# The last batch's projections in another order, over 89 steps instead of 64

## The chip, the cores and the metric

The kernel runs on one core of a Trainium2 chip. That core has five engines that run their own instruction streams and meet only at semaphores: TensorE (PE; its weight loads are listed apart as PEld), VectorE (DVE), ScalarE (ACT), GpSimd (POOL) and SyncE (SP), which here issues DMAs. The metric is the device time of one execution in microseconds, lower is better.

## The reference

One transformer block with adaptive modulation, in float32: 4 batches of 1024 tokens, width 512, 16 heads of 32.

```python
ada = silu(c) @ Wada.T + bada                      # six vectors of 512 for each batch
h = rmsnorm(x, g1) * (1 + scale_msa) + shift_msa
q, k, v = split(h @ Wqkv.T + bqkv)                 # 16 heads of 32
q, k = rmsnorm(q, gq) * 32**-0.5, rmsnorm(k, gk)   # over the 32 of a head
x = x + gate_msa * ((softmax(q @ k.T) @ v) @ Wproj.T + bproj)
h = rmsnorm(x, g2) * (1 + scale_mlp) + shift_mlp
x = x + gate_mlp * (gelu(h @ Wfc1.T + bfc1) @ Wfc2.T + bfc2)
```

## The kernel before, in words

There are three stages: a short setup, the attention, and then output projection and MLP. The change is in the attention alone, which writes its result to DRAM for the third stage.

**The steps.** The attention is a loop over 256 steps, the same on every engine (`for L in range(START, AFTER)`; 18 steps ahead of step 0 only prepare). The 16 heads are taken in 4 groups of 4 (`g`). A batch is 64 steps, a group of heads 16, and the two halves of its queries 8 each; in this text a half is such a run of 8 steps, and `j` (0 to 7) is the place in it, one block of 128 keys. Batch 3, the last, is attended in steps 192 to 255. In a step TensorE makes the scores of 4 heads in two pairs (L456), ScalarE takes the exponential of each pair into one of 3 `probs` buffers (L616, two instructions of 128x1024), TensorE multiplies the `probs` of the step before with `v` (L469), and VectorE adds the `probs` of the step before to a running sum (L681, 128x2048; seven times in a half, none for the first block alone). At `j` = 1 TensorE sums the rows of the finished half (`row_sums`, L486) and waits for its seventh addition. From there the sums go through DRAM, are inverted on VectorE at `j` = 5 (L701), come back by DMA (L403), and at `j` = 0 the half's output is scaled (`output`, L697).

**The projections.** The products of a batch's `h` with the weights of q, k and v are not a stage of their own: they are put between the scores. They are 24 products for each batch: 8 tiles of `v` (`v_of(t, steps)`) and 16 units (`k_of(g, half, steps)`, `q_of(g, half, steps)`), one for each group, half, and q or k. Each product is 12 matmuls of 512 columns into the one PSUM bank `gemm` (L521 for units, L534 for `v`). `placed` lays them out one after the other: a product of 3 steps gets 4 of its 12 matmuls in each step, one of 2 steps 6, one of 6 steps 2. `fill(L, 0)` issues the first part of a step's share between the two pairs of scores, `fill(L, 1)` the second part behind them. In a new product `fill` first waits until VectorE has copied the previous one out of the bank (`gemm_free`).

**What follows a unit.** One step behind the end of a unit VectorE copies it to `raw` with its bias (`raw_out`, L712; a tile of `v` is copied by `v_out`, L722), ScalarE squares it (L597), the step after that TensorE adds the squares up for each head (`sum_squares`, L493, moved on by a step where another user of its bank stands), ScalarE takes logarithm and inverse root (L587, L591), and VectorE makes the normalised unit in two parts (`make_parts`, L761, L767, L769), at the END of its step, behind that step's addition. `raw_out`, `v_out`, `output` and the inversion stand AHEAD of the addition. SyncE stores the parts to DRAM (L359) and loads them, spread for the scores, at places that the group and the half fix (L381). Every engine works its stream in order.

**The input.** Eight tiles of `x` for each batch are normalised and turned, one every 8 steps, the last of batch 3 at step 170; ScalarE and GpSimd split the turned tile in two parts two steps later (L607, L653). A product of the second half of the tokens needs all 8 tiles.

**The plan.** `PLAN` is a list of numbers that sets all of this; from `FILL`, `UNIT_END` and `VOUT` every engine derives its stream. For the batches 2 and 3 it begins 48 steps ahead of the batch and lasts 64 steps, so the products of batch 3 lie in the steps 144 to 207, and the steps 208 to 255 have none.

Of the kernel before, what the change touches and what calls it, by code (L numbers as in the profile page):

```python
# [23 lines left out]
B, T, D = 4, 1024, 512  # L24
# [11 lines left out]
BSTEPS = NG * STEPS  # L36
# [18 lines left out]
def v_of(t, steps):  # L55
    return "v", 0, t, steps


def k_of(g, half, steps):
    return "k", g, half, steps  # L60


def q_of(g, half, steps):
    return "q", g, half, steps


def placed(step, b, products):

    plan = []
    for kind, g, x, steps in products:  # L70
        plan.append((step, steps, b, kind, g, x))
        step += steps
    return plan


def first_half(v_steps, steps):

    return [p for g in range(NG) for p in (k_of(g, 0, steps), q_of(g, 0, steps), v_of(g, v_steps))]


SECOND_HALF = [k_of(0, 1, 3), q_of(0, 1, 3), v_of(4, 2), v_of(5, 2), k_of(1, 1, 3), v_of(6, 2), q_of(1, 1, 3),
               k_of(2, 1, 3), v_of(7, 2), q_of(2, 1, 3), k_of(3, 1, 3), q_of(3, 1, 3)]
START = -18
PLAN = placed(-14, 0, [v_of(0, 1), v_of(1, 1), v_of(2, 1), k_of(0, 0, 1), q_of(0, 0, 1), v_of(3, 1), v_of(4, 1),
                       k_of(0, 1, 1), q_of(0, 1, 1), v_of(5, 1), v_of(6, 1), v_of(7, 1)])
# [2 lines left out]
PLAN += placed(25, 1, [v_of(0, 2), v_of(1, 2), k_of(0, 0, 2), q_of(0, 0, 2), k_of(1, 0, 2), v_of(2, 2), q_of(1, 0, 2), k_of(2, 0, 2),  # L88
                       q_of(2, 0, 2), v_of(3, 2), k_of(3, 0, 3), q_of(3, 0, 3), k_of(0, 1, 2), q_of(0, 1, 2), v_of(4, 2), v_of(5, 2),
                       k_of(1, 1, 3), v_of(6, 2), q_of(1, 1, 3), k_of(2, 1, 2), v_of(7, 2), q_of(2, 1, 3), k_of(3, 1, 3), q_of(3, 1, 3)])  # L90
for b in range(2, B):
    PLAN += placed(BSTEPS * b - 48, b, first_half(2, 3) + SECOND_HALF)

FILL = {step + i: (kind, b, g, x, i, steps) for step, steps, b, kind, g, x in PLAN for i in range(steps)}
UNIT = [(b, g, kind, x) for _, _, b, kind, g, x in PLAN if kind != "v"]
# [31 lines left out]
for step, n in FIN_AT.items():  # L127
    b, g, kind, half = UNIT[n]
# [1255 lines left out]
```

## Time and profile before

| | us |
|---|---|
| median of 3 runs (1860.57 to 1865.57) | 1863.95 |
| the profiled execution | 1864.95 |
| its span in the trace | 1863.2 |
| first exponential of step 144, and of step 208 | 650.25, 877.94 |
| start of the last pair of exponentials | 999.4 |
| TensorE busy, of the span | 1760.5 (94%) |
| VectorE busy | 1101.3 (59%) |
| ScalarE busy | 921.3 (49%) |

A step can be read from the trace by the start of its first exponential (ACT L616): from one such start to the next is the step's length. An engine's busy share over the whole span is an average of three stages. For the attention it says little, since the third stage keeps TensorE busy and the others less so.

### The profile page before, as it was taken

The page shows a single profiled execution, that of the slowest core. Times are in us where ns is not written, and L with a number is a line of the kernel's source. Part 1 is how long each engine was busy: PE and PEld are TensorE (multiplying, and loading weights), DVE is VectorE, ACT ScalarE, POOL GpSimd, SP SyncE. Part 2 cuts the span into 40 slices and gives each one's busy share as a digit, 9 for nine tenths or more (in the row PEclk, how much of TensorE's full clock was granted, in tenths as well). Part 3 has the DMA queues.
Part 4 walks back from the last instruction along what each step waited for, and adds up shares of the span by engine and source line. Part 5 has one row for each costly group of instructions (what it writes and reads, how often), then busy time and mean ns, then how long its engine had stood idle before and what let it go on. Part 6 is the DMA issues. An engine that isn't in the chain of part 4 may idle for free. (4 is left out here: it accounts for less than half of the span.)

```text
span 1863.2 us, 23267 instructions
## 1 busy us (share of the span) xinstructions
PE 1760.5 (94%) x8368; PEld 1139.4 (61%) x8368; DVE 1101.3 (59%) x1343; ACT 921.3 (49%) x1110; POOL 363.3 (19%) x296
## 2 busy tenths in 40 slices
PE   3899899999999999999995799999999999999998
PEld 1555454555555555544231577888888787878786
DVE  4578878888898888878785654223232414232311
ACT  2277577777777777777885432222121222122221
POOL 1100100010110110000000432324241424233331
PEclk7999999999999999999997799999999999999999
DMA  5555535556555555454563331202020201001000
GB/s 184 153 146 142 138 107 139 137 138 157 132 132 144 135 144 128 126 133 137 132 134 103 116 102 40 63 6 62 17 62 17 62 17 51 28 30 44 6 29 23
DMA packets 137611, 176.69 MB, mean 95 GB/s; under 512 B 33668, under 2 KB 58244, under 8 KB 137528
## 3 DMA queue, kind: packets, MB, share of 16 engines
q1 hardware_dynamic: 122472, 158.79, 32.1%
q10 hardware_dynamic: 15056, 16.81, 2.8%
q8 instruction: 50, 0.82, 0.2%
q14 instruction: 33, 0.27, 0.1%
HBM read 124.63 MB, written 50.92 MB: 94 GB/s over the span
## 5 line engine op out<-in xcount | busy, mean ns | idle before, releaser
L616 ACT ACTIVATE probs<-scores,shift 128x1024 f32<-128x1024 f32 x512 | 549.7, 1115 | 195.6 <-PE scores L456 191.8
L681 DVE TENSOR_TENSOR sums<-sums,probs 128x2048 f32<-128x2048 f32 x192 | 444.5, 2315 | 45.0 <-ACT probs L616 40.7
L456 PE MATMUL scores<-q_stack,k_stack 128*128 128x512 f32 x1024 | 345.7, 423 | 6.6 <-ACT probs L616 6.5
L456 PEld LDWEIGHTS scores<-q_stack,k_stack 128*128 128x128 f32 x1024 | 169.6, 188 | 254.4 <-ACT probs L616 133.3
L1148 PE MATMUL acc<-w_hi,act_parts 128*128 128x512 f32 x1024 | 317.4, 391 | 0.0
L469 PE MATMUL pv<-probs,v 128*32 128x512 f32 x2048 | 274.3, 608 | 0.4 <-ACT probs L616 0.4
L1111 POOL TENSOR_TENSOR act_parts<-act_full,act_parts 128x512 fp32r<-128x512 f32 x128 | 169.6, 1325 | 501.7 <-ACT act_parts L1062 501.0
L1055 ACT ACTIVATE act_full<-up,f_bias 128x512 f32<-128x512 f32 x128 | 88.3, 690 | 337.7 <-PE up L1165 317.0
L1148 PEld LDWEIGHTS acc<-w_hi,act_parts 128*128 128x128 f32 x1024 | 190.7, 188 | 38.6
L1165 PE MATMUL up<-z_hi,w_hi 128*128 128x512 f32 x512 | 201.5, 394 | 5.1 <-POOL z_lo L1098 5.1
L1165 PE MATMUL up<-z_lo,w_hi 128*128 128x512 f32 x512 | 200.3, 391 | 0.0
L1165 PE MATMUL up<-z_hi,w_lo 128*128 128x512 f32 x512 | 200.2, 391 | 0.0
L1148 PE MATMUL acc<-w_lo,act_parts 128*128 128x512 f32 x512 | 199.4, 389 | 0.0
L1223 DVE TENSOR_TENSOR y_next<-proj,p_bias 128x512 f32<-128x512 f32 x28 | 19.3, 690 | 297.2 <-PE proj L1126 297.2
L1062 ACT ACTIVATE act_parts<-act_full 128x512 fp32r<-128x512 f32 x128 | 81.2, 635 | 222.1 <-PE acc L1148 221.0
L521 PE MATMUL gemm<-h_hi,wqkv_hi 128*128 128x512 f32 x256 | 103.9, 406 | 14.4 <-issue 11.6
L1165 PEld LDWEIGHTS up<-z_hi,w_hi 128*128 128x128 f32 x512 | 96.9, 189 | 25.5 <-POOL z_lo L1098 5.5
L469 PEld LDWEIGHTS pv<-probs,v 128*32 128x32 f32 x2048 | 41.1, 108 | 114.7 <-ACT probs L616 62.2
L658 POOL TENSOR_TENSOR x_inv<-x_sqc,minus_half 128x1 f32<-128x1 f32 x32 | 17.6, 551 | 475.9 <-DVE x_sqc L733 475.9
L1165 PEld LDWEIGHTS up<-z_lo,w_hi 128*128 128x128 f32 x512 | 97.0, 189 | 20.1
L1165 PEld LDWEIGHTS up<-z_hi,w_lo 128*128 128x128 f32 x512 | 96.8, 189 | 20.4
L1148 PEld LDWEIGHTS acc<-w_lo,act_parts 128*128 128x128 f32 x512 | 96.1, 188 | 20.2
(134 smaller groups left out, 2092.9 us busy)
## 6 DMA issues: line engine op xcount, KB each, us to landing
parts_scratch<-parts SPq DMA_DIRECT2D x64, 512.0 KB, 3.1
k_stack<-parts_scratch SPq DMA_DIRECT2D x128, 256.0 KB, 4.9
q_stack<-parts_scratch SPq DMA_DIRECT2D x128, 256.0 KB, 5.1
xt<-in_x SPq DMA_DIRECT2D x32, 256.0 KB, 2.9
heads_out<-o_out SPq DMA_DIRECT2D x32, 256.0 KB, 4.7
out<-result SPq DMA_DIRECT2D x32, 256.0 KB, 2.0
inverse<-inverse_scratch SPq DMA_DIRECT2D x124, 64.0 KB, 2.0
heads<-heads_out SPq DMA_DIRECT2D x30, 256.0 KB, 3.3
```

The lines of the kernel that those rows point to most:

```text
L456: mm = nc.tensor.matmul(scores[p][:, i, :], k_stack[s][:, h, j * P:(j + 1) * P], q_stack[half][:, h, :], start=True, stop=True)
L469: mm = nc.tensor.matmul(pv[hh % NH][h * DH:(h + 1) * DH, :], v[b % 2][:, j, (g * HG + h) * DH:(g * HG + h + 1) * DH], probs[l % RING][:, h ...
L521: mm = nc.tensor.matmul(gemm[:], w[:, k, at:at + P], h[:, k, c], start=(n == 0), stop=(n == len(terms) - 1))
L616: nc.scalar.activation(probs[L % RING][:, 2 * p:2 * p + 2, :], scores[p][:], ACT.Exp, bias=small["shift"][:]).then_inc(exp_done, 1)
L658: nc.gpsimd.tensor_tensor(x_inv[:, t:t + 1], x_sqc[:, t:t + 1], small["minus_half"][:, 0:1], ALU.pow).then_inc(inv_done, 1)
L681: nc.vector.tensor_tensor(sums[:], a[:], probs[l % RING][:], ALU.add).then_inc(added, 1)
L1055: nc.scalar.activation(act_full[m % 2][:], up[m % 2][:], ACT.Gelu_apprx_tanh, bias=f1_bias[:, m:m + 1]).then_inc(gelu_done, 1)
L1062: nc.scalar.activation(act_parts[m % 2][:, 0, :], act_full[m % 2][:], ACT.Copy).then_inc(act_hi, 1)
L1111: nc.gpsimd.tensor_tensor(act_parts[m % 2][:, 1, :], act_full[m % 2][:], full(act_parts[m % 2][:, 0, :]), ALU.subtract).then_inc(act_lo, 1)
L1148: mm = nc.tensor.matmul(acc[t][:], act_parts[m % 2][:, b, t * P:(t + 1) * P], w2[a][:, m, :], start=(m == 0 and i == 0), stop=(m == NM - 1 ...
L1165: mm = nc.tensor.matmul(up[m % 2][:], w1[a][:, k, m * P:(m + 1) * P], z[b][:, k, :], start=(k == 0 and i == 0), stop=(k == KT - 1 and i == 2))
L1223: nc.vector.tensor_tensor(yt, proj[:], p_bias[:], ALU.add).then_inc(proj_moved, 1)
```

## The change

The batches 0, 1 and 2 keep their plan. Batch 3 gets one of its own. It begins at the same step (144), takes the products in another order, gives 12 tiles and units other numbers of steps, leaves the steps 171 and 172 free, and ends at step 232 instead of 207. The tiles of `v` come earlier (the last ends at step 181, before at 198), and the units of the groups 2 and 3 now lie at the steps 194 to 232, inside the batch. From step 188 on all units of q and the first unit of k of group 2 are six steps long.

```diff
-for b in range(2, B):
-    PLAN += placed(BSTEPS * b - 48, b, first_half(2, 3) + SECOND_HALF)
+PLAN += placed(2 * BSTEPS - 48, 2, first_half(2, 3) + SECOND_HALF)
...
+PLAN += placed(3 * BSTEPS - 48, 3, [k_of(0, 0, 3), v_of(0, 3), q_of(0, 0, 3), v_of(1, 3), v_of(2, 3), v_of(3, 3), k_of(1, 0, 3),
...
+PLAN += placed(3 * BSTEPS - 19, 3, [k_of(0, 1, 3), q_of(0, 1, 3), v_of(7, 3), q_of(1, 0, 3), k_of(1, 1, 3), q_of(1, 1, 6),
+                                    k_of(2, 0, 6), q_of(2, 0, 6), k_of(2, 1, 3), q_of(2, 1, 6),
+                                    k_of(3, 0, 3), q_of(3, 0, 6), k_of(3, 1, 3), q_of(3, 1, 6)])
```

In the whole, counted from the two plans for the 112 steps 144 to 255:

| matmuls of products in a step | steps before | steps after |
|---|---|---|
| 6 | 16 | 6 |
| 4 | 48 | 45 |
| 2 | 0 | 36 |
| 0 | 48 | 25 |

Both columns hold 288 matmuls. What moves on TensorE shows in two pieces. `scores0` and `scores1` are the two pairs of scores, `gemm` the bank of the products, `aux` that of the sums, `pv` the output. Before, TensorE at step 203:

```order
L456 MATMUL scores0<-q_stack1,k_stack0 128x512 x2
L521 MATMUL gemm<-h_lo,wqkv_hi 128x512
L521 MATMUL gemm<-h_hi,wqkv_lo 128x512
L456 MATMUL scores1<-q_stack1,k_stack0 128x512 x2
L521 MATMUL gemm<-h_hi,wqkv_hi 128x512
L521 MATMUL gemm<-h_lo,wqkv_hi 128x512
L493 MATMUL aux<-squares,head_ones 128x512
L469 MATMUL pv1<-probs1,v1 32x512 x4
```

After, TensorE at the steps 218 and 219 (its lines are six higher in number):

```order
L462 MATMUL scores0<-q_stack1,k_stack1 128x512 x2
L527 MATMUL gemm<-h_hi,wqkv_hi 128x512
L462 MATMUL scores1<-q_stack1,k_stack1 128x512 x2
L527 MATMUL gemm<-h_lo,wqkv_hi 128x512
L475 MATMUL pv1<-probs1,v1 32x512 x4
L462 MATMUL scores0<-q_stack1,k_stack1 128x512 x2
L527 MATMUL gemm<-h_hi,wqkv_lo 128x512
L462 MATMUL scores1<-q_stack1,k_stack1 128x512 x2
L527 MATMUL gemm<-h_hi,wqkv_hi 128x512
L499 MATMUL aux<-squares,head_ones 128x512
L475 MATMUL pv1<-probs2,v1 32x512 x4
```

A step of a six-step unit holds one matmul of the product behind each pair of scores, where a step of a three-step unit holds two.

On VectorE the neighbours of the copies change. `raw` is the copy of a unit, `parts` its normalised form, `sums` the addition. Before, VectorE at the steps 200 to 205:

```order
L697 TENSOR_TENSOR o_out<-pv1,inverse 128x512
L681 TENSOR_TENSOR sums<-sums,probs1 128x2048
L761 SCALAR_TENSOR_TENSOR raw0<-norms,raw0 128x512
L767 TENSOR_SCALAR parts<-raw0 128x512
L769 SCALAR_TENSOR_TENSOR parts<-raw0,parts 128x512
L712 TENSOR_SCALAR raw1<-gemm,qk_bias 128x512
L681 TENSOR_TENSOR sums<-probs2,probs0 128x2048
L681 TENSOR_TENSOR sums<-sums,probs1 128x2048
L681 TENSOR_TENSOR sums<-sums,probs2 128x2048
L712 TENSOR_SCALAR raw0<-gemm,qk_bias 128x512
L701 RECIPROCAL compact<-compact 128x16
L681 TENSOR_TENSOR sums<-sums,probs0 128x2048
```

After, VectorE at the steps 200 to 206:

```order
L718 TENSOR_SCALAR raw0<-gemm,qk_bias 128x512
L703 TENSOR_TENSOR o_out<-pv1,inverse 128x512
L687 TENSOR_TENSOR sums<-sums,probs1 128x2048
L687 TENSOR_TENSOR sums<-probs2,probs0 128x2048
L687 TENSOR_TENSOR sums<-sums,probs1 128x2048
L687 TENSOR_TENSOR sums<-sums,probs2 128x2048
L767 SCALAR_TENSOR_TENSOR raw0<-norms,raw0 128x512
L773 TENSOR_SCALAR parts<-raw0 128x512
L775 SCALAR_TENSOR_TENSOR parts<-raw0,parts 128x512
L707 RECIPROCAL compact<-compact 128x16
L687 TENSOR_TENSOR sums<-sums,probs0 128x2048
L718 TENSOR_SCALAR raw1<-gemm,qk_bias 128x512
```

Before, the three instructions of `make_parts` are at step 200 and the next copy at step 202, and no addition stands between them, since step 201 has none. After, they are at step 204, and an inversion and an addition stand between them and the copy of step 206.

## Rows read from the trace of the kernel before

**Rows 1.** Windows: length; busy us and count by engine; PEclk, DMA share, GB/s

```profile
650.25:877.94 227.69, 226.96 (x1170) 115.78 (x1168) 189.51 (x177) 171.44 (x189) 11.79 (x8) 1.00 0.51 133
877.94:999.50 121.56, 114.83 (x620) 38.31 (x622) 101.13 (x59) 105.27 (x105) 0.00 (x0) 0.99 0.50 119
```

**Rows 2.** Waits of TensorE from 650.25 to 877.94: in total, times, longest

```profile
PE scores L456 <- ACT probs L616: 0.7, 1, 0.7
```

**Rows 3.** Timeline of ScalarE, steps with products: start, length, instructions, [idle before]

```profile
794.38 2.18 ACT L616 ACTIVATE probs<-scores,shift 128x1024 f32<-128x1024 f32 x2 [1.05 <-PE scores L456]
...
797.86 2.20 ACT L616 ACTIVATE probs<-scores,shift 128x1024 f32<-128x1024 f32 x2 [0.69 <-PE scores L456]
...
802.59 2.12 ACT L616 ACTIVATE probs<-scores,shift 128x1024 f32<-128x1024 f32 x2 [2.02 <-PE scores L456]
805.62 2.12 ACT L616 ACTIVATE probs<-scores,shift 128x1024 f32<-128x1024 f32 x2 [0.91 <-PE scores L456]
808.66 2.12 ACT L616 ACTIVATE probs<-scores,shift 128x1024 f32<-128x1024 f32 x2 [0.92 <-PE scores L456]
...
832.90 2.12 ACT L616 ACTIVATE probs<-scores,shift 128x1024 f32<-128x1024 f32 x2 [0.41 <-PE scores L456]
...
836.80 2.12 ACT L616 ACTIVATE probs<-scores,shift 128x1024 f32<-128x1024 f32 x2 [1.05 <-PE scores L456]
```

**Rows 4.** Timeline of ScalarE, steps 224 to 229, without products

```profile
922.49 4.24 ACT L616 ACTIVATE probs<-scores,shift 128x1024 f32<-128x1024 f32 x4 [0.44 <-DVE sums L681]
...
928.03 4.25 ACT L616 ACTIVATE probs<-scores,shift 128x1024 f32<-128x1024 f32 x4 [0.82 <-PE scores L456]
...
932.72 4.25 ACT L616 ACTIVATE probs<-scores,shift 128x1024 f32<-128x1024 f32 x4 [0.44 <-PE scores L456]
```

**Rows 5.** Timeline, steps 187 to 189: addition, copy, next product's first weights

```profile
807.77 2.29 DVE L681 TENSOR_TENSOR sums<-sums,probs 128x2048 f32<-128x2048 f32 x1 [0.74 <-ACT probs L616]
...
809.98 0.75 DVE L712 TENSOR_SCALAR raw<-gemm,qk_bias 128x512 f32<-128x512 f32 x1
...
811.19 0.19 PEld L534 LDWEIGHTS gemm<-wqkv_hi,h_hi 128*128 128x128 f32 x1
```

**Rows 6.** Timeline, steps 212 to 218: VectorE, and who waited for it

```profile
890.83 0.68 DVE L761 SCALAR_TENSOR_TENSOR raw<-norms,raw 128x512 f32<-128x512 f32 x1
...
892.74 0.25 DVE L701 RECIPROCAL compact<-compact 128x16 f32<-128x16 f32 x1
892.90 7.02 DVE L681 TENSOR_TENSOR sums<-sums,probs 128x2048 f32<-128x2048 f32 x3
901.11 0.69 DVE L697 TENSOR_TENSOR o_out<-pv,inverse 128x512 f32<-128x512 f32 x1 [1.19 <-DMA inverse<-inverse_scratch]
901.72 2.28 DVE L681 TENSOR_TENSOR sums<-sums,probs 128x2048 f32<-128x2048 f32 x1
904.05 1.93 PE L486 MATMUL aux<-sums,ones 128*32 128x512 f32 x8 [2.38 <-DVE sums L681]
908.43 4.25 ACT L616 ACTIVATE probs<-scores,shift 128x1024 f32<-128x1024 f32 x4 [1.78 <-DVE sums L681]
```

**Rows 7.** Timeline, steps 29 and 30: a copy behind `make_parts`

```profile
218.38 1.12 ACT L616 ACTIVATE probs<-scores,shift 128x1024 f32<-128x1024 f32 x1 [0.79 <-PE scores L456]
219.46 0.68 DVE L722 TENSOR_TENSOR v<-gemm,v_bias 128x512 f32<-128x512 f32 x1
...
220.19 0.50 PE L521 MATMUL gemm<-h_hi,wqkv_hi 128*128 128x512 f32 x1 [1.93 <-DVE v L722]
...
225.62 1.12 ACT L616 ACTIVATE probs<-scores,shift 128x1024 f32<-128x1024 f32 x1 [2.78 <-PE scores L456]
```

**Rows 8.** Windows over two places behind a wait (columns of Rows 1)

```profile
904.00:907.40 3.40, 3.35 (x16) 0.59 (x16) 1.28 (x1) 0.60 (x1) 0.00 (x0) 0.51 0.67 158
...
221.40:224.80 3.40, 3.40 (x13) 0.93 (x12) 2.94 (x2) 1.12 (x1) 0.00 (x0) 0.50 0.34 112
```

**Rows 9.** Timeline: the split of batch 3's last tile at step 172

```profile
751.66 2.68 POOL L653 TENSOR_TENSOR h_lo<-h_full,h_hi 128x512 fp32r<-128x512 f32 x1 [7.79 <-ACT h_hi L607]
```

More of the change, by code:

```diff
@@ L90 @@
                        k_of(1, 1, 3), v_of(6, 2), q_of(1, 1, 3), k_of(2, 1, 2), v_of(7, 2), q_of(2, 1, 3), k_of(3, 1, 3), q_of(3, 1, 3)])
-for b in range(2, B):
-    PLAN += placed(BSTEPS * b - 48, b, first_half(2, 3) + SECOND_HALF)
+PLAN += placed(2 * BSTEPS - 48, 2, first_half(2, 3) + SECOND_HALF)
+PLAN += placed(3 * BSTEPS - 48, 3, [k_of(0, 0, 3), v_of(0, 3), q_of(0, 0, 3), v_of(1, 3), v_of(2, 3), v_of(3, 3), k_of(1, 0, 3),
+                                    v_of(4, 2), v_of(5, 2), v_of(6, 2)])
+PLAN += placed(3 * BSTEPS - 19, 3, [k_of(0, 1, 3), q_of(0, 1, 3), v_of(7, 3), q_of(1, 0, 3), k_of(1, 1, 3), q_of(1, 1, 6),
+                                    k_of(2, 0, 6), q_of(2, 0, 6), k_of(2, 1, 3), q_of(2, 1, 6),
+                                    k_of(3, 0, 3), q_of(3, 0, 6), k_of(3, 1, 3), q_of(3, 1, 6)])
 FILL = {step + i: (kind, b, g, x, i, steps) for step, steps, b, kind, g, x in PLAN for i in range(steps)}
```

## The prediction

> **What bounds the kernel now.** I read the windows first, to see which engine is full in the stretch that the change touches, then TensorE's waits there, then ScalarE's timeline, because the start of a step's first exponential dates every step. The steps 144 to 207, with products, take 227.69 us, and TensorE is busy for 226.96 of them; the steps 208 to 255, without, take 121.56, with TensorE at 114.83 at almost full clock [rows 1]. A busy TensorE is not a full one, so the waits decide: in the first stretch it waited once, for 0.7 us [rows 2]. There it sets the pace, and each matmul costs its time.
>
> Prices of steps, from start to start [rows 3]: with 4 matmuls of products 805.62 to 808.66, 3.03 (mean with the step before, 802.59 to 805.62); with 6, 794.38 to 797.86, 3.48. So a matmul more costs 0.45/2 = 0.225 us. A sum of squares adds 0.87 (832.90 to 836.80 is 3.90, less 3.03), a row sum 1.25 (797.86 to 802.59 is 4.73, less 3.48). Without products two steps take 932.72 - 928.03 = 4.69, so 2.345 each, and with a row sum in one of them 928.03 - 922.49 = 5.54, 0.85 more [rows 4]. TensorE's own work in an empty step would be 3.03 - 4 x 0.225 = 2.13; the 0.2 above it is the loop of scores, exponential and next scores.
>
> **A step with two matmuls.** The trace has none. TensorE's work makes it 2.13 + 0.45 = 2.58. From below the bound is the empty step, 2.345, from above the one with four, 3.03. I take 2.58, since the slope is measured between four and six in a stretch without waits.
>
> The Trainium skill, TensorE: Matmul & The Clock Gate, section "Wait — 56ns, not 53.3ns?", gives a start-to-start time of 215.7 ns for 512 columns at full clock. The steps of rows 3 give 225 here, so the rows' value stands. By the page's the balance below would be about 4 us of gain instead of 5.
>
> **The balance of the plan.** Before, the 112 steps hold 16 with six matmuls, 48 with four, 48 with none: 16 x 3.48 + 48 x 3.03 + 48 x 2.345 = 313.7. After, 6, 45, 36 with two and 25 with none: 20.9 + 136.4 + 92.9 + 58.6 = 308.7. That is 5.0 us less. Sums of squares, row sums and turns are as many in both and almost all lie in steps with products. With the bounds of the two-matmul step the balance runs from 13.4 less to 11.2 more (36 steps by -0.235 or +0.45).
>
> **A wait that the plan adds on GpSimd.** The first unit of the second half of tokens starts at step 173, three steps earlier than before, and needs the last tile's second part. Its split stands ahead of step 172's exponentials, takes 2.68 us on GpSimd [rows 9], and the steps 171 and 172 are now empty, so about 2.0 us pass until step 173's first weights. I count 0.7 us, once, between 0 and 1.5.
>
> **What VectorE does to the lighter steps.** This is the part that I weigh most. VectorE's addition of a step can start when its second exponential has ended, 2.15 after the step's start (805.62 to 807.77), and takes 2.29; three in a row take 7.02, 2.34 each [rows 3, 5, 6]. `make_parts` stands behind an addition and takes 892.74 - 890.83 = 1.9 [rows 6]. So each unit puts VectorE 1.9 behind. It makes that up by the difference of the step and 2.34: 0.69 in a step with four matmuls, 0.24 in one with two. A half's start (`j` = 0 is not added) gives back 2.3, a sum of squares or row sum about 1 more.
>
> The copy out of the bank comes at the head of its step, behind the addition of the step before. In steps of 3.03 it ends at 809.98 + 0.75 = 810.73, and the next product's weights go at 811.19, 0.5 ahead of that step's start [rows 5]: 0.46 in hand. In steps of 2.58 an addition in time ends 2.15 - 2.58 + 2.29 = 1.86 after the start of the step ahead of the copy's, the copy at 2.61, and the weights are due at 2.58 - 0.5 = 2.08: 0.5 late even without `make_parts`.
>
> Place B, in full, from the start of step 204: the addition of step 203 starts at 2.15 - 2.58 = -0.43 and the next thing follows at +1.91. `make_parts` to 3.8, inversion to 4.0, addition to 6.34, copy (0.75) to 7.1. The first weights of step 206 are due at 2 x 2.58 - 0.5 = 4.66. TensorE waits 2.4. This is the place that the two pieces of VectorE's order show. What is queued behind: the second pair of scores of step 206, and so the second exponential, `pv`, and all else.
>
> The same sum for the other places where a copy comes two or three light steps behind `make_parts`, without a half's start between: step 200 (behind 197), 9.25 against 7.24, 2.0; step 215 (behind 212) 2.1; step 224 (behind 218 and 221) 2.4. With B 8.9.
>
> A row sum waits in the same way for the seventh addition. After steps without products the trace has one: 1.9 of `make_parts`, 1.19 of DMA and 0.6 of `output` ahead of the addition, 3.7 together, made TensorE wait 2.38 [rows 6], so 1.3 is in hand. Before the row sum of step 233 VectorE has `make_parts` at 228 and 230 and ends 2.7 late, 1.4 of wait; before that of 193 (`make_parts` at 188 and 191) 2.3 late, 0.9 to 1.0. With 0.9: 2.3.
>
> In steps with four matmuls a few pairs are new too: copies at 153, 159, 169 and 185 behind `make_parts` at 150, 157, 168 and 182, with 0.75, 0.85, 0.5 and 0.85 late, and at 182 about 0.1: 3.0. Before, the copies of such steps had a half's start or two longer steps ahead, and rows 2 show none of these waits.
>
> Together 14.2 us of waits. Bounds: none below, if VectorE's backlog is taken up somewhere that I don't see; above, 20, if each also delays the exponentials' chain.
>
> **The clock.** Two waits of this size are in the trace. At step 29 TensorE waited 1.93 for a copy behind `make_parts`, and in the 3.4 us behind it the granted clock was 0.50, the lower level, 1.2 GHz. The step took 225.62 - 218.38 = 7.24 against 3.48 of an undisturbed one: 3.8 more, of which I put 2.0 to the wait and 1.8 to the clock [rows 7, 8]. At 904.00 it was again at 0.51, behind the wait of 2.38 [rows 6, 8]. Of the four long waits I let one be followed by such a fall: 1.8 (none to four, 0 to 7.2).
>
> The Trainium skill speaks for less here (same page, section "Why this matters for your kernels"): its rule is that idle gaps between bursts make the clock fall, and steady activity keeps it. Rows 8 agree in kind: it fell behind waits, not in the empty steps, where TensorE has least to do. By the rule alone, fuller steps would save the clock.
>
> **The stall of step 217.** Its cause, `make_parts` at `j` = 4 of an empty half, is found again: the last unit's now stands at step 236, also `j` = 4, with inversion and row sum behind it at 237 and 241. So it moves and isn't gained: 0. Its price is 4.1 (7.5 against 3.4), kept for the range.
>
> **Sum.** Against the profiled execution's 1864.95: -5.0 + 0.7 + 14.2 + 1.8 = +11.7, 1876.6. The median of the runs shown is 1.0 below that execution, so 1875.6. Nothing else moves: loads of the stacks stand at the same steps, setup and third stage are the same.
>
> **Rivals.**
> 1. The balance wins. VectorE is busy for 189.51 of 227.69 [rows 1], so 17% of it is free; if TensorE's waits come to less than the 5 us of the balance, the time is -5.0 + 0.7 + 3 of small waits, 1863, and 1860 with none; with the stall of 217 gone too, 1857 to 1859. For it: in total VectorE has the time. Against: it works in order, and rows 6 and 7 show that a backlog is not made up before it is asked for. It decides where waits stay under 4.3.
> 2. They cancel: waits of 3 to 9, no fall of the clock. 1864 to 1869. For it: one of my places may be off by a step's slack each, 0.5 x 9 places.
> 3. The falls of the clock multiply: all four long waits are followed by one, each making the next steps late. 1864 + 9.9 + 7.2, 1881. For: both waits of rows 6 and 7 had one. Against: those are two cases, and rows 1 show no fall elsewhere in the stretch.
>
> **Chances.** My forecast 0.45, rival 3 0.17, rival 2 0.20, rival 1 0.18. What a measurement can tell is 0.3%, 5.6 us: faster below 1858.4, slower above 1869.5. Two thirds of rival 1 end below 1858.4, the rest of it and rival 2 in between: faster 0.12, same 0.26, slower 0.62. The range 1860 to 1883 takes in the cancelled case and most of rival 3; the likeliest case by itself is 1870 to 1880.
>
> **What would show it.** In the profile after: a group of waits of TensorE for `raw` (L718) or `v` (L728) of 8 to 12 us in the steps 144 to 232, where now there is none; steps 206, 215, 200 and 224 of some 5 us; steps of two matmuls at 2.58 between them; a wait of some 2.4 us at step 241, and none at 217; the steps 144 to 255 about 10 us longer. Wrong it would be if the light steps run at 2.58 without waits for copies, or at another length than 2.5 to 2.7.

## The result, and the profile after

| | before | after |
|---|---|---|
| median (8 runs each) | 1863.29 | 1869.36 |
| lowest to highest | 1860.57 to 1865.83 | 1867.57 to 1871.36 |
| the profiled execution | 1864.95 | 1867.57 |
| first exponential of step 144 to that of step 255 | 348.12 | 354.07 |
| of these: steps 144 to 191, and 192 to 254 | 172.33, 175.79 | 165.95, 188.12 |

The changed kernel takes 1.0034 times as long, 95% interval 1.0024 to 1.0044: slower by 6.1 us. 1875.6 was predicted, 11.7 more than before, so the sign was right, and about half of the size. 1869.36 lies in the range of 1860 to 1883, but just below the likeliest case (1870 to 1880), and below the 1869.5 above which the prediction counted a kernel as slower.

The changed stretch alone accounts for it: 354.07 - 348.12 = +5.95. The two profiled executions differ by only 2.6: the stretch starts 1.9 us later in that of before, of which 1.6 are step 29 with a fall of the clock [rows 7, 8] that the other lacks, and behind the stretch it takes 1.4 more. So the comparison is made step by step inside the stretch. The windows first, columns as in rows 1. Before:

```profile
650.25:998.37 348.12, 340.71 (x1782) 153.64 (x1780) 289.61 (x234) 275.58 (x291) 11.79 (x8) 1.00 0.51 128
```

After:

```profile
648.35:1002.42 354.07, 339.68 (x1782) 153.81 (x1780) 287.69 (x234) 274.29 (x291) 11.85 (x8) 1.00 0.50 126
```

No engine works longer by more than 0.2 us, and the counts are the same. TensorE's busy time falls by 1.0 and the stretch grows by 6: it waits. The starts of ScalarE's exponentials, to be read as in rows 3, say where:

```profile
835.33 2.12 ACT L622 ACTIVATE probs<-scores,shift 128x1024 f32<-128x1024 f32 x2 [0.48 <-PE scores L462]
837.92 1.11 ACT L622 ACTIVATE probs<-scores,shift 128x1024 f32<-128x1024 f32 x1 [0.47 <-PE scores L462]
840.23 1.11 ACT L622 ACTIVATE probs<-scores,shift 128x1024 f32<-128x1024 f32 x1 [1.20 <-PE scores L462]
...
842.20 2.12 ACT L622 ACTIVATE probs<-scores,shift 128x1024 f32<-128x1024 f32 x2 [0.33 <-PE scores L462]
...
857.16 1.11 ACT L622 ACTIVATE probs<-scores,shift 128x1024 f32<-128x1024 f32 x1 [0.47 <-PE scores L462]
...
862.12 2.12 ACT L622 ACTIVATE probs<-scores,shift 128x1024 f32<-128x1024 f32 x2 [0.56 <-PE scores L462]
...
886.67 1.11 ACT L622 ACTIVATE probs<-scores,shift 128x1024 f32<-128x1024 f32 x1 [0.47 <-PE scores L462]
...
891.42 2.12 ACT L622 ACTIVATE probs<-scores,shift 128x1024 f32<-128x1024 f32 x2 [0.56 <-PE scores L462]
...
915.93 1.11 ACT L622 ACTIVATE probs<-scores,shift 128x1024 f32<-128x1024 f32 x1 [0.47 <-PE scores L462]
...
920.60 2.12 ACT L622 ACTIVATE probs<-scores,shift 128x1024 f32<-128x1024 f32 x2 [0.56 <-PE scores L462]
```

Step 199, with two matmuls, takes 837.92 - 835.33 = 2.59: the undisturbed light step is what was predicted. Step 200 takes 4.28, step 206 4.96, step 215 4.75, step 224 4.67. An `x1` where the steps around show `x2` is a mark of its own: the second exponential didn't follow the first, since its scores stood behind a wait between the two pairs. (Another instruction of ScalarE between the two prints as `x1` too, so the length of the step decides.) The timeline of VectorE and TensorE over the steps 204 to 206 gives the cause:

```profile
853.78 0.69 DVE L767 SCALAR_TENSOR_TENSOR raw<-norms,raw 128x512 f32<-128x512 f32 x1
...
855.57 0.24 DVE L707 RECIPROCAL compact<-compact 128x16 f32<-128x16 f32 x1
...
855.73 2.23 DVE L687 TENSOR_TENSOR sums<-sums,probs 128x2048 f32<-128x2048 f32 x1
...
857.88 0.74 DVE L718 TENSOR_SCALAR raw<-gemm,qk_bias 128x512 f32<-128x512 f32 x1
...
858.72 0.47 PE L527 MATMUL gemm<-h_hi,wqkv_hi 128*128 128x512 f32 x1 [1.67 <-issue]
```

`make_parts`, inversion, addition and copy follow without a gap, and the next product starts 0.1 behind the copy's end (857.88 + 0.74). The profile labels this wait "issue". TensorE's waits from 640 to 1000, as total, times and longest, show it so too:

```profile
PE gemm L527 <- issue: 6.0, 4, 1.7
PE aux L492 <- DVE sums L687: 3.2, 3, 1.4
...
PE gemm L527 <- POOL h_lo L659: 1.2, 1, 1.2
...
```

Whoever looks for a group named `raw` finds none. The four waits (1.46, 1.67, 1.47 and 1.39 us, at the steps 200, 206, 215 and 224) are each on a copy, which shows by what ended just before. The other two groups are the late row sums and step 173. The kernel before has such waits too, ahead of the stretch; from 94 to 600:

```profile
PE gemm L521 <- issue: 9.8, 7, 2.3
PE gemm L521 <- DVE v L722: 2.1, 2, 1.9
```

The stall of step 217 did move to step 241, smaller:

```profile
964.32 4.23 ACT L622 ACTIVATE probs<-scores,shift 128x1024 f32<-128x1024 f32 x4 [0.45 <-PE scores L462]
...
966.31 2.28 DVE L687 TENSOR_TENSOR sums<-sums,probs 128x2048 f32<-128x2048 f32 x1
...
968.65 1.06 PE L492 MATMUL aux<-sums,ones 128*32 128x512 f32 x8 [1.42 <-DVE sums L687]
...
971.34 2.12 ACT L622 ACTIVATE probs<-scores,shift 128x1024 f32<-128x1024 f32 x2 [0.97 <-PE scores L462]
```

The steps 240 and 241 take 7.02 together; step 241 takes 4.91, where step 217 took 7.54 before. Here `output` found its DMA landed, while at 901.11 it waited 1.19 for it [rows 6], and the clock didn't fall.

### The profile page after: what moved, and what is told of

Read it like the earlier page. It is cut to its first block and busy times, and to the rows that moved or that the text cites. A ratio compares the mean times of both kernels' runs of the same rounds, so it can differ in the third digit from the quotient of the medians.

```text
span 1865.8 us, 23267 instructions
## 1 busy us (share of the span) xinstructions
PE 1757.4 (94%) x8368; PEld 1138.5 (61%) x8368; DVE 1098.6 (59%) x1343; ACT 918.8 (49%) x1110; POOL 363.9 (20%) x296
```

## The experiments

Twelve kernels ran, in three groups, each with the kernel before beside it. The changes of a kernel are told against the changed kernel, unless "before" is named. The theory is VectorE's backlog: it works in order, `make_parts` puts it 1.9 behind, a light step gives back only 0.24, and TensorE can't start a product until the copy. Its rivals are the one bank (a copy doesn't fit between two products of light steps, whatever VectorE has done) and a loss in the order or in the light steps themselves.

**`make_parts` behind the copy, four units.**

```diff
+LATER = {55: 201, 56: 206, 58: 216, 60: 225}
+FIN_AT = {LATER.get(n, step): n for step, n in FIN_AT.items()}
```

> The changed plan, with make_parts of four units moved behind the next copy out of the bank: the units copied at 194, 200, 209 and 218 get it at the steps 201, 206, 216 and 225 instead of 197, 204, 212 and 221. No work is added or taken away. Theory (VectorE's backlog): the four long steps fall from 4.28, 4.95, 4.75 and 4.67 us to 2.6, 3.0, 3.0 and 3.0, 7.0 us together, so 1862.4. Rival (the one bank: in a light step the copy itself does not fit between two products): the four steps stay long, by 0.5 us or more each as worked out for a copy without backlog, or as long as they are; 1867 to 1869. Rival (the loss lies elsewhere, in the light steps or the order): 1869, whatever the four steps do.

1864.75 (11 runs; 1.0011 of before, 1.0002 to 1.0020). The four steps fell to 3.00, 3.50, 3.44 and 3.45, by 5.3 us. About 0.4 stayed in each. The timeline at step 200:

```profile
834.75 2.29 DVE L689 TENSOR_TENSOR sums<-sums,probs 128x2048 f32<-128x2048 f32 x1 [0.25 <-ACT probs L624]
...
836.96 0.74 DVE L720 TENSOR_SCALAR raw<-gemm,qk_bias 128x512 f32<-128x512 f32 x1
...
837.76 2.13 ACT L624 ACTIVATE probs<-scores,shift 128x1024 f32<-128x1024 f32 x2 [0.47 <-PE scores L464]
837.78 0.19 PEld L529 LDWEIGHTS gemm<-h_hi,wqkv_hi 128*128 128x128 f32 x1 [0.57 <-issue]
...
840.76 1.11 ACT L624 ACTIVATE probs<-scores,shift 128x1024 f32<-128x1024 f32 x1 [0.35 <-PE scores L464]
```

The copy waits only for an addition in time (834.75 + 2.29 = 837.04), and is still 0.5 late for the weights: what was worked out for a copy without backlog. The 7.0 of the expectation had left it out. The rival "the loss lies elsewhere" has fallen; of the one bank 1.7 of 7.0 us could be true. The total is 2.4 above the 1862.4 expected, of which this is 1.7.

The same run shows the price of a fall of the clock. Its row sum of step 241 had the wait of the changed kernel, 1.41, and the clock fell; first the timeline, then a window with the columns of rows 1:

```profile
958.85 4.25 ACT L624 ACTIVATE probs<-scores,shift 128x1024 f32<-128x1024 f32 x4 [0.44 <-PE scores L464]
...
963.16 1.84 PE L494 MATMUL aux<-sums,ones 128*32 128x512 f32 x8 [1.41 <-DVE sums L689]
...
967.52 4.25 ACT L624 ACTIVATE probs<-scores,shift 128x1024 f32<-128x1024 f32 x4 [1.87 <-DVE sums L689]
```

The window behind that wait:

```profile
963.30:966.70 3.40, 3.40 (x17) 0.51 (x12) 1.58 (x1) 0.60 (x1) 0.00 (x0) 0.50 0.38 98
```

The steps 240 and 241 take 8.67, against 7.02: the fall to the lower level, 1.2 GHz, costs 1.65.

**Half of the additions.** Which of the two is it that keeps the 0.4? From step 144 on this kernel leaves out the sums of two of the four heads of a group.

```diff
-                nc.vector.tensor_tensor(sums[:], a[:], probs[l % RING][:], ALU.add).then_inc(added, 1)
+                w = slice(0, HG // 2) if l >= 144 else slice(0, HG)
+                nc.vector.tensor_tensor(sums[:, w, :], a[:, w, :], probs[l % RING][:, w, :], ALU.add).then_inc(added, 1)
```

> The changed plan, in which the additions on VectorE cover only two of the four heads of a group from step 144 on (128x1024 instead of 128x2048; the sums of the other two heads are left out). All other instructions and all waits stay. Backlog theory: VectorE is then free whenever a product ends, so all waits for copies go, also the 0.4 us that the steps 200, 206, 215 and 224 kept when make_parts was moved behind the copy: 2.6, 3.0, 3.0 and 3.0 us; the row sums of 193, 233 and 241 fall to 3.8, 3.0 to 3.4 and 3.4. With 7.0 + 2.3 + 1.4 + 1.5 us gone: 1857. The one-bank rival: 0.4 us stays in each of the four steps, 1.7 together, since the copy's own 0.75 does not fit there. The wait for GpSimd at step 173 (1.4) stays by both.

1854.10 (5 runs; 0.9945 of before, 0.9931 to 0.9958). ScalarE at the steps 200 and 206:

```profile
835.49 2.12 ACT L622 ACTIVATE probs<-scores,shift 128x1024 f32<-128x1024 f32 x2 [0.46 <-PE scores L462]
...
838.07 1.11 ACT L622 ACTIVATE probs<-scores,shift 128x1024 f32<-128x1024 f32 x1
...
853.03 2.12 ACT L622 ACTIVATE probs<-scores,shift 128x1024 f32<-128x1024 f32 x2 [0.46 <-PE scores L462]
...
856.07 1.12 ACT L622 ACTIVATE probs<-scores,shift 128x1024 f32<-128x1024 f32 x1 [0.41 <-PE scores L462]
```

2.58 and 3.04, and 3.05 at 215 and 224: all four clean. `make_parts` stands where it stood. So a copy does fit behind one bank, and the 0.4 too is VectorE's, an addition of 2.3 in a step of 2.58. The row sums are on time as well (step 193 3.78, 233 3.01, 241 3.42). The stretch takes 339.50, 14.6 less than in the changed kernel, where 12.2 were expected. The surplus lies at two places. The steps 148 to 150 take 9.98 instead of 10.86, and, against the expectation, the wait of step 173 shrank as well, from 1.4 to 0.35. GpSimd's split is shorter. Its row, first of the changed kernel, then of this one, then of this one for the tile of step 156, with no addition beside it:

```profile
748.82 2.86 POOL L659 TENSOR_TENSOR h_lo<-h_full,h_hi 128x512 fp32r<-128x512 f32 x1 [10.38 <-ACT h_hi L613]
```

```profile
748.64 1.82 POOL L659 TENSOR_TENSOR h_lo<-h_full,h_hi 128x512 fp32r<-128x512 f32 x1 [10.99 <-ACT h_hi L613]
```

```profile
692.98 1.29 POOL L659 TENSOR_TENSOR h_lo<-h_full,h_hi 128x512 fp32r<-128x512 f32 x1 [10.74 <-ACT h_hi L613]
```

**`make_parts` nearer to the copy, three units.**

```diff
+LATER = {55: 199, 58: 214, 60: 223}
```

> The changed plan, with make_parts of three units two steps nearer to the next copy: at 199, 214 and 223 instead of 197, 212 and 221. Backlog theory: in a light step VectorE makes up 2.58 - 2.34 = 0.24 us, so two fewer of them make each of the waits of the steps 200, 215 and 224 longer by 0.48: 4.76, 5.23 and 5.15 us instead of 4.28, 4.75 and 4.67. The one-bank rival: no change in these steps.

1875.77, one run. Step 200 took 6.21, step 215 6.76, step 224 5.22. The timeline of step 200:

```profile
839.72 1.11 ACT L624 ACTIVATE probs<-scores,shift 128x1024 f32<-128x1024 f32 x1 [0.47 <-PE scores L464]
...
840.82 0.74 DVE L720 TENSOR_SCALAR raw<-gemm,qk_bias 128x512 f32<-128x512 f32 x1
...
841.66 0.47 PE L529 MATMUL gemm<-h_hi,wqkv_hi 128*128 128x512 f32 x1 [2.07 <-issue]
...
845.93 2.12 ACT L624 ACTIVATE probs<-scores,shift 128x1024 f32<-128x1024 f32 x2 [1.65 <-PE scores L464]
```

The windows behind that wait and of step 224:

```profile
842.90:846.30 3.40, 3.40 (x12) 1.45 (x9) 1.46 (x1) 1.75 (x3) 0.00 (x0) 0.50 1.01 249
923.44:928.66 5.22, 3.39 (x18) 1.93 (x19) 4.49 (x5) 2.75 (x4) 0.00 (x0) 1.00 0.62 184
```

The wait of step 200 grew from 1.46 to 2.07, 0.6 where 0.48 was expected, and step 224, whose clock stayed up, by 0.55. The rest at 200 and 215 is the clock (also at 206, 6.53, which this kernel doesn't touch). So the dose acts as the theory says, and the total is worse than it said, for three falls. With one run, the total itself says little; the steps are what counts here.

**`make_parts` behind the next copy or row sum, eleven units.**

```diff
+LATER = {55: 201, 56: 206, 58: 216, 60: 225, 48: 153, 49: 161, 50: 169, 52: 185, 54: 193, 62: 233, 63: 241}
```

> The changed plan, with make_parts of eleven units moved behind the next copy or row sum (the four of the other run, and at 150 to 153, 157 to 161, 168 to 169, 182 to 185, 191 to 193, 230 to 233, 236 to 241). Backlog theory: besides the 7.0 us of the four steps it takes 1.1 from step 153, 0.5 from 157 to 159, 0.4 from 169, 0.3 from 185, 0.8 from 193, 0.6 from 233 and 1.5 from 241: 12.2 us less than the changed kernel, 1857.2, about 6 us below the kernel before. The one-bank rival: 1865 to 1869.

1858.42 (8 runs; 0.9975 of before, 0.9964 to 0.9985): 11 us below the changed kernel. The stretch takes 343.15. Steps 153, 185, 193, 233 and 241 are at 4.24, 4.24, 3.78, 3.00 and 3.42, without their waits. 10.9 us are gained where 12.2 were expected: the 0.4 at each of the four copies stays, as in the kernel with four units.

**Without the two empty steps.**

```diff
-                                    v_of(4, 2), v_of(5, 2), v_of(6, 2)])
+                                    v_of(4, 3), v_of(5, 3), v_of(6, 2)])
```

> The changed plan without the two empty steps 171 and 172: two tiles of v get three steps instead of two, all else stays. It tests the wait of step 173 for GpSimd's second part of the last tile (1.4 us in the changed kernel's profile). If that is the cause, step 173 falls from 4.45 to 3.03. The plan has 2 steps with none and 4 with six fewer and 6 with four more: 6 x 3.03 - 4 x 3.48 - 2 x 2.345 = 0.4 less needed than it costs now, so about 1.8 us in all less, with 0.4 off the waits of 169: 1867.5.

1868.67 (12 runs; 1.0027 of before, 1.0018 to 1.0035); the 1867.5 expected lies within the interval, but so does nearly no gain at all, and the steps decide. Step 173 fell from 4.45 to 3.06 and the steps 144 to 191 from 165.95 to 163.77, 2.2 less. In its profile step 206 had the fall that the changed kernel's lacked; the exponentials of it:

```profile
856.38 1.11 ACT L622 ACTIVATE probs<-scores,shift 128x1024 f32<-128x1024 f32 x1 [0.47 <-PE scores L462]
...
862.85 2.12 ACT L622 ACTIVATE probs<-scores,shift 128x1024 f32<-128x1024 f32 x2 [2.08 <-PE scores L462]
```

The window between the two:

```profile
858.90:862.30 3.40, 3.40 (x12) 1.02 (x11) 3.12 (x2) 1.63 (x2) 0.00 (x0) 0.50 0.72 196
```

6.47 against 4.96, 1.5 for the clock (the waits: 1.65 here, 1.67 there). The same wait is followed by a fall in one execution and not in another.

**Both remedies.**

> Both remedies together: make_parts behind the next copy or row sum for the eleven units, and no empty steps 171 and 172. Backlog theory and the GpSimd wait add up: 12.2 and 1.8 less than the changed kernel, 1855.4, which is 8 us below the kernel before. If the two overlap or the waits move elsewhere, 1857 to 1860.

1856.12 (6 runs; 0.9953 of before, 0.9941 to 0.9966), the lowest median of those that leave nothing out, and near the 1855.4 expected; the stretch takes 341.32.

**The stall of 217, in the kernel before.**

```diff
+LATER = {63: 217}
```

> The kernel before, with make_parts of its last unit moved from step 212 (j = 4) to 217 (j = 1, the step without an addition). It tests what the stall of step 217 is. Backlog theory: the 7.5 us of step 217 become 3.4, with the wait of 2.4 for the row sum and the fall of the clock behind it both gone: 4.1 less, 1859.2. If the wait is that of the output's DMA (the inverse rows' load behind other stores) and not of make_parts: 1.2 stays, 1861 or more. If the fall of the clock there comes by chance and not behind the wait: 2.4 less, 1860.9.

1858.24 (8 runs; 0.9970, 0.9959 to 0.9980). The exponentials of the steps 216 and 218, with step 217 between them, and `output`:

```profile
899.49 0.68 DVE L699 TENSOR_TENSOR o_out<-pv,inverse 128x512 f32<-128x512 f32 x1
...
899.82 4.24 ACT L618 ACTIVATE probs<-scores,shift 128x1024 f32<-128x1024 f32 x4 [0.55 <-PE scores L458]
...
905.35 2.12 ACT L618 ACTIVATE probs<-scores,shift 128x1024 f32<-128x1024 f32 x2 [0.81 <-PE scores L458]
```

The steps 216 and 217 take 5.53, step 217 alone 3.42. The whole 4.1 is gone, the wait for the DMA and the fall with it. The DMA's delay hangs on `make_parts` too: its store of `parts` no longer goes just ahead of the store of the inverted sums, and that store lands 1.4 us after its issue (892.18 to 893.60) instead of 4.5 (893.27 to 897.81). One `make_parts` in the wrong place cost the kernel before 0.3%.

**The order at the old pace.** Units three steps, `v` two, products end at step 207.

```diff
+PLAN += placed(3 * BSTEPS - 48, 3, [k_of(0, 0, 3), v_of(0, 2), q_of(0, 0, 3), v_of(1, 2), v_of(2, 2), v_of(3, 2), k_of(1, 0, 3),
+                                    q_of(1, 0, 3), k_of(2, 0, 3), v_of(4, 2), v_of(5, 2), v_of(6, 2)])
...
```

> The new order (v early, units by need) at the old pace: three steps for a unit, two for a tile of v, so that the products end at step 207 as before and there are no steps with two matmuls. The balance of the plan is then the same as before, 0. If the order is to blame for the loss: 1866 to 1869. If the light steps are: 1863 plus 1 to 3 us of waits of new neighbours in steps with four matmuls (copies at 152, 167 and 179), so 1864 to 1866.

1865.96 (11 runs; 1.0015, 1.0006 to 1.0024). The total lies where the two expectations meet, and can't choose between them. The steps can: 144 to 191 take 175.23 against 172.33, and from 192 on it is the kernel before (175.96 against 175.79). So at the old pace the order alone costs about 3 us, and new neighbours make waits there too; at step 152, `make_parts` two steps ahead:

```profile
679.84 0.75 DVE L717 TENSOR_SCALAR raw<-gemm,qk_bias 128x512 f32<-128x512 f32 x1
...
680.68 0.47 PE L539 MATMUL gemm<-wqkv_hi,h_hi 128*128 128x512 f32 x1 [1.14 <-issue]
```

**The pace in the old order.** Last three units six steps each.

```diff
+PLAN += placed(3 * BSTEPS - 48, 3, first_half(2, 3) + SECOND_HALF[:-3] + [q_of(2, 1, 6), k_of(3, 1, 6), q_of(3, 1, 6)])
```

> The old order, with the last three units stretched to six steps each (199 to 216): 18 steps with two matmuls in the place of 9 with four and 9 with none. By the prices 9 x 3.03 + 9 x 2.345 - 18 x 2.58 = 1.9 us less. No make_parts lies two or three light steps ahead of a copy here, so the backlog theory expects the whole gain but 0.5 us at the row sum of step 217: 1861.8. If light steps cost more in themselves, or the one bank is to blame: 2 copies in the light stretch at 0.5 or more, 1863 to 1865.

1860.38 (11 runs; 0.9987, 0.9978 to 0.9996). A gain, though the interval's end is near 1. The stretch takes 344.36, 3.8 less than before, where 1.4 was expected. The other 2.4 come from the stall: the steps 217 and 225 take 3.62 and 4.91 instead of 7.54 and 3.43, so it shrinks as it moves, as in the changed kernel. Step 205 is at 2.97, 0.4 late.

> The old order, last three units stretched to six steps, and make_parts of the last unit at step 225 (j = 1, no addition) instead of 220 (j = 4). Against the stretched kernel: step 225 falls from 4.91 to 3.4, 1.5 less, 1858.9. Against the kernel before with the same remedy (1858.2 in its run, 0.9970 of the kernel before): if the stretch itself is worth its balance of 1.9 less 0.4 at the copy of step 205 and 0.4 for the row sums of 209 and 217, 1.1 below it, about 0.9964; if stretching only hid the stall of step 217, the same 0.9970.

(`LATER = {63: 225}` added.) 1858.37 (8 runs; 0.9973, 0.9962 to 0.9983), not to be told from before with its own remedy (0.9970). Inside the stretch it takes 342.94 against 343.89, 0.95 less, near the 1.1 expected, but too little for the total to show.

**The sums in a row at 84 and 148.**

```diff
+for n in (32, 48):
+    step = next(k for k, m in SUM_AT.items() if m == n)
+    del SUM_AT[step]
+    SUM_AT[step + 1] = n
```

> The kernel before with two remedies and the old plan: make_parts of the last unit at step 217 instead of 212, and the second of the two sums of squares in a row in the steps 84 and 148 moved on by one step (with its logarithm and make_parts). In the traces the steps 84 and 148 take 5.73 us, since ScalarE's logarithm waits for make_parts of the unit before, behind an addition. Backlog theory: 5.73 + 2.61 + 2.9 falls to 3.03 + 3.9 + 3.5, 0.8 to 0.9 less at each of the two places: 1858.2 - 1.7 = 1856.5. Rival (the wait moves one step on, as the neighbour changes): 1858.

1858.19 (7 runs; 0.9972, 0.9960 to 0.9983), no change. Step 148 fell from 5.73 to 3.06, but 149 and 150 rose from 2.61 and 2.90 to 3.89 and 4.22: 11.24 became 11.17. The expectation had put step 150 at 3.5. It is 0.7 dearer, since the moved `make_parts` now stands ahead of the copy there and the copy is late; of this kernel:

```profile
672.31 0.75 DVE L720 TENSOR_SCALAR raw<-gemm,qk_bias 128x512 f32<-128x512 f32 x1
...
673.16 0.47 PE L542 MATMUL gemm<-wqkv_hi,h_hi 128*128 128x512 f32 x1 [0.48 <-issue]
```

So what came true is the rival, that the wait moves one step on with the neighbour. It isn't all work that has to be done: with half of the additions these three steps took 0.9 less.

> The changed plan with all remedies: make_parts of eleven units behind the next copy or row sum, no empty steps 171 and 172, and the second of the two sums of squares in a row at the steps 84 and 148 moved on by one. Against the kernel with the first two (0.9953 of the kernel before): 1.7 less again, 1854.4, 0.9944. Rival as in the other run: no change, 0.9953. If the new plan is worth its balance once its waits are gone, this is 2 us below the old plan with the same remedies.

1857.56 (6 runs; 0.9968, 0.9956 to 0.9980). It is 0.4 shorter in the stretch than the kernel with both remedies (340.90): here step 150 takes 3.51, and the steps 148 to 150 take 10.46 instead of 10.86. Its total can't be told from that one's.

## Why the sign was right and the size twice too large

The mechanism is shown: the waits follow the place of `make_parts` and the length of the additions, in both directions (the kernels with four units, eleven units, three units nearer and half of the additions). The terms, each as the lengths of the steps give it (a disturbed step less its length where it is undisturbed):

| term | predicted | measured |
|---|---|---|
| balance of the plan (measured: the remainder) | -5.0 | -3.9 |
| step 173, GpSimd | 0.7 | 1.4 |
| copies at 200, 206, 215, 224 | 8.9 | 6.9 |
| row sums of 193, 233 | 2.3 | 1.9 |
| copies in steps with four or six matmuls | 3.0 | 2.3 |
| falls of the clock | 1.8 | 0 |
| the stall of 217 | 0 | -2.6 |
| sum | 11.7 | 6.0 |

- **What bounds the kernel, and the price of a light step**: right. 2.54 to 2.62 measured, 2.58 predicted. The slope of 0.225 us for a matmul held (3.03 - 2.58 for two), against the 215.7 ns that the Trainium skill gives (TensorE: Matmul & The Clock Gate, section "Wait — 56ns, not 53.3ns?").
- **The balance**: the step that failed is "almost all lie in steps with products" in both. The row sums of 209, 217 and 225 lay in empty steps before, at 0.85, and lie in steps with products after, at 1.2 (step 209: 3.02 before, 3.79 after, 0.77 more, where the step itself is dearer by 0.24 only). That is about 1.1, the whole difference of the two balances. The -3.9 is not measured by itself, but what remains of 5.95. (Eleven products changed their number of steps, not twelve; the counts of the steps were right.)
- **The copies**: the places were all right, also the four in fuller steps (153 1.1, 157 to 159 0.5, 169 0.4, 185 0.3), the sizes not. At place B, the copy was put at 7.1 after the start of step 204 and ended at 858.62 - 852.04 = 6.6. `make_parts` took 1.79 instead of 1.9 and started 0.17 earlier, and between addition and copy lie 2.15, not 2.34. 0.3 to 0.8 at each of the four places make up the 2.0.
- **The row sums**: 0.85 at step 193 (4.63 against 3.78) and 1.0 at 233 (4.03 against 3.00 in the kernel with eleven units), where 0.9 and 1.4 were put.
- **Step 173**: GpSimd's split took 2.86, not 2.68, and from its start to the first weights of step 173 only 1.5 were free, 0.5 less than reckoned.
- **The clock**: both waits that I had looked at were followed by a fall, and I counted one in four. The trace of before holds more: in the steps 0 to 254 TensorE waited 1.3 us or more seven times (steps 17, 23, 29, 39, 48, 53 and 217), and falls came behind three of them (23, 29 and 217), while the 2.28 of step 48 had none. In the changed kernel's profile none followed, in that of the kernel without empty steps one did (1.5), in another it followed a wait of only 1.4 (1.65). As a price 1.8 was a little high: step 29 takes 5.68 in the changed kernel's profile, where no fall follows the same wait, against 7.24 in that of before, 1.6 more. Whether a fall comes does not hang on the plan. Whether the other runs of the changed kernel, all slower than the profiled one, had falls in the stretch is not shown. The exponentials of the steps 29 and 30 in the changed kernel:

```profile
218.07 1.11 ACT L622 ACTIVATE probs<-scores,shift 128x1024 f32<-128x1024 f32 x1 [0.79 <-PE scores L462]
...
223.75 2.19 ACT L622 ACTIVATE probs<-scores,shift 128x1024 f32<-128x1024 f32 x2 [1.30 <-PE scores L462]
```

- **The stall of 217**: "it moves and isn't gained" is the step that failed most, by 2.6. Of 4.1 only the backlog moved (1.5). The DMA's delay and the clock's fall stayed behind. Why the inverse rows landed in time at 240 (2.54 from store to the next load's issue, 961.68 - 959.14, against 897.83 - 893.27 = 4.56 before, with a store of `parts` 0.4 ahead in both) isn't settled: about 2.5 is the usual time so close behind such a store, and the 4.56 is what is odd; in the order at the old pace, with the unit where it was, the delay was there again.

That the sum came out at half, and not further off, is partly luck. The balance and step 173 were put 1.8 too low together, all other terms 7.5 too high. The time lies between my case and rival 2 (waits of 3 to 9, 1864 to 1869). Rival 2's reason is not what happened: the waits of the new plan came to 12.5, and what brought the time near it is the stall of 217. Rival 3 had its three falls in the kernel with three units nearer, and none in the changed kernel's profile.

Rival 1, that the balance wins, came out false for this plan. With the two remedies it comes out true in the stretch: 341.32, against 343.89 of the old plan with its own remedy, 2.6 less. The intervals of the two totals overlap (0.9941 to 0.9966, 0.9959 to 0.9980), so this rests on the steps of one profile each.

## What to carry to other kernels

In an order written by hand, count for each filler not only the engine that it fills but the distance between what it leaves on the next engine and the next thing waited for there. Thinning out the work of the engine that bounds a stage takes away, step by step, the slack in which its helpers catch up; the average load (VectorE 81% here) doesn't show that. Place the long helper work right BEHIND what others wait for, in the steps where the helper has least to do; that was worth 11 us here, where the new plan alone cost 6. Check each new place for the next neighbour: at step 148 the wait only moved on.

## What the runs showed of the hardware

- A fall of the granted clock to its lower level costs 1.5 to 1.65 us here (the same step with and without it: step 29, 7.24 and 5.68; step 206, 6.47 and 4.96; step 241, 6.55 and 4.91). It comes behind some of TensorE's waits and not behind others of the same length. At step 29 all 14 traces have a wait of 1.92 to 1.95; in seven a fall follows and the step takes 7.23 to 7.28, in seven none does and it takes 5.67 to 5.70. The shortest wait with a fall was 1.41 (step 241); the changed kernel's waits of 1.39 to 1.67 in the stretch had none.
- GpSimd's subtraction of 128x512 took 2.86 us beside VectorE's additions of 128x2048, 1.82 beside one of 128x1024, and 1.29 with none beside it; VectorE's own addition beside the first took 3.04 instead of 2.29. The two engines slow each other down, and a wait for GpSimd depends on what VectorE does just then.
- An 8 KB store to DRAM (of the inverted sums) landed 1.4 us after its issue, in the median of the 336 in the 14 traces that had no store of `parts` in the 3 us ahead of them. With one of 512 KB less than 0.7 us ahead it took 2.5 to 2.6, in 38 of 41; the 4.5 of the half of step 212, in the kernel before and in that with the order at the old pace, are the exceptions.
